# Second attention of a two-layer block: exponentials in a cycle of three tiles, value groups issued several steps later

## The chip, the cores and the metric

The kernel runs on 1 core of one Trainium2 chip. The metric is the device time of the whole program in microseconds (us). Of the core's engines this case concerns PE (TensorE, matrix products), DVE (VectorE), ACT (ScalarE) and SP (SyncE, which only issues DMAs here).

## The reference

The input is 4 batches of 512 tokens with 256 features. Each of two layers normalises the tokens, runs an attention and a mixture of experts on them, and adds both to the tokens. The change concerns the attention of the second layer, a grouped attention with 8 groups of keys and values, 4 query heads per group, and 8 features per head:

```python
q = q.reshape(Bx, Sx, N_GROUPS, R, HEAD_DIM).transpose(0, 2, 3, 1, 4)
k = k.reshape(Bx, Sx, N_GROUPS, HEAD_DIM).transpose(0, 2, 1, 3)
v = v.reshape(Bx, Sx, N_GROUPS, HEAD_DIM).transpose(0, 2, 1, 3)
sim = jnp.einsum('bgrsd,bgtd->bgrst', q, k) / math.sqrt(HEAD_DIM)
attn = jax.nn.softmax(sim, axis=-1)
out = jnp.einsum('bgrst,bgtd->bgrsd', attn, v)
```

With 4 batches and 8 groups there are 32 pairs (b, g). Each needs 4 heads x 512 queries x 512 keys of scores, their maxima over the keys, exponentials, and the product with the values.

## The kernel before

The second attention is one pipeline of stages, written out by hand. Stage (b, s) works on several groups at once: the scores of group s, the exponentials of group s-1, and the outputs of group s-2. Stage (b, 8) and (b, 9) take the scores of groups 0 and 1 of the next batch, so that the program runs through the stages (0,0) to (0,9), (1,2) to (1,9), (2,2) to (2,9), (3,2) to (3,8). A stage has 16 steps. The instructions of each engine run in the order in which they are written; semaphores order the engines against each other.

What PE issues in a stage, by its helper and its line:

- `scores` (L812), one matmul (128 queries x 512 keys) in each of the 16 steps. I call them S0 to S15. DVE takes the maximum of each with one reduction (L1690).
- `maxima_t` (L848), four transposes of the maxima of group s-1 (I call it MX), issued at the step `turn["maxima"]`. DVE adds the result to the stacked queries, `qm` (L1683).
- `scores_t` (L821), items ST0 to ST7 of group s-1: two matmuls each, the scores with the keys on the partitions and the maxima already subtracted. ACT turns each item into exponentials with one ACTIVATE (L1198), E0 to E7. Two items fill one tile `pt[t]`.
- `values` (L833), groups V0 to V3: V_t multiplies tile t of exponentials with the values, 4 matmuls per group (8 records in the trace), and adds up in PSUM bank 7. After V3, ACT copies bank 7 to `ot` (`outputs`, the COPY at L992).
- `outputs_t` (L841), four transposes of `ot` (OUT), issued at the step `turn["outputs"]`. DVE then divides by the sums: a reciprocal and a product (L1660, L1662; I call the pair N).
- In stages 5, 6 and 7 of batches 0 to 2, at step 13, `project` (L539 to L541), six matmuls for the next batch. ACT adds the bias (`compact`, L1171, or L1174 and L1176 for the keys) and DVE makes the low part (L1646, L1649). In stage 9, `values_by_key` (L804) transposes the values of the next batch.

Two tables say at which step the items of a group are issued, counted from the first step of the stage in which its exponentials begin; steps from 16 on fall into the next stage:

```python
            TRANSPOSED = (4, 6, 7, 8, 11, 13, 15, 17)
            VALUED = (10, 15, 19, 19)
```

Three resources couple the engines. PSUM banks 0 to 2 are a ring (`next_bank`) that scores, MX, OUT, projection and `values_by_key` take in PE's order; each use waits until DVE has read the use three places before it. ST items alternate between two pairs of banks, so item i waits for exponential i-2. And the exponentials of tile t may be written only when the value group that read this buffer before is done.

Small steps of the routing of the second layer (masks and slots) are spread over DVE's order in the stages of batch 0, and GpSimd dispatches tokens during the later batches.

Of the kernel before, what the change touches and what calls it, by code (L numbers as in the profile page):

```python
# [7 lines left out]
P = 128  # L8
B, S, H = 4, 512, 256
# [3 lines left out]
QT = S // P  # L13
# [16 lines left out]
NG, R, HD = 8, 4, 8  # L30
# [11 lines left out]
def program(nc, x_in, aw0_in, aw1_in, ws0_in, moe0_in, moe1_in, pad_in, const_in, bias_in, out):  # L42
# [3 lines left out]
    with ctx:  # L46
# [9 lines left out]
        SM, M = 4096, 6688  # L56
# [137 lines left out]
        va = tf(QT, NG, 32)  # L194
        pt = [tf(R, S) for _ in range(2)]
        ot = tf(S)
# [101 lines left out]
        def turns(s, following):  # L298
            never = QT * R
            return {"maxima": 1, "outputs": 6, "values": 4 if s == NG + 1 else never,  # L300
                    "project": 13 if following and NG - 3 <= s < NG else never}
# [235 lines left out]
        def _(pe):  # L537
# [287 lines left out]
            def values(b, g, t):  # L825

                pe.wait_ge(b_ex, b * (2 * NQ) + ((g * QT + t) * 2 + 2))
                if t == 0 and g >= 1:
                    pe.wait_ge(b_ot, b * NG + g)
                if t == 0 and g % NG == 0:  # L830
                    pe.wait_ge(b_va, b + (g // NG + 1))
                for r in range(R):
                    ins = nc.tensor.matmul(psum[32 * r:32 * r + 32, 7, :], va[:, t, g % NG, :], pt[t % 2][:, r, :],  # L833
                                           start=(t == 0), stop=(t == QT - 1), tile_position=(0, 32 * r))
                ins.then_inc(b_pv, 1)
# [16 lines left out]

            TRANSPOSED = (4, 6, 7, 8, 11, 13, 15, 17)
            VALUED = (10, 15, 19, 19)

# [134 lines left out]
        def _(act):  # L990
# [194 lines left out]
            def stage(b, s, last):  # L1185
                back, following = s >= 1, not last and s >= 1
                if s >= 2:
                    outputs(b, s - 2)
                for t in range(QT):
                    if isinstance(b, int) and (b, s, t) == (0, 2, 1):  # L1190
                        gating_exp(E1, 2, TT)
                    if back:
                        g = s - 1
                        for h in range(2):
                            act.wait_ge(b_st, b * (2 * NG * QT) + ((g * QT + t) * 2 + h + 1))
                            if g * QT + t >= 2:
                                act.wait_ge(b_pv, b * (NG * QT) + (g * QT + t - 1))
                            nc.scalar.activation(pt[t % 2][:, 2 * h:2 * h + 2, :], psum[:, 3 + 2 * h:5 + 2 * h, :],  # L1198
                                                 ACT.Exp, scale=float(HD) ** -0.5).then_inc(b_ex, 1)
# [658 lines left out]
```

## Time and profile before

| | |
|---|---|
| median of 3 runs | 1185.54 us |
| lowest, highest | 1183.62, 1187.75 us |
| profiled execution, its own time | 1182.18 us |
| span of the profiled execution | 1180.4 us |
| second attention in it (first MX to last value group) | 501.86 to 963.97 us |
| an ordinary stage (MX to MX) | 13.5 us |
| mean granted TensorE clock | 0.956 of full speed |

The profile lists, for each engine, how long instructions were recorded as busy, and what ended each idle stretch ("idle before <-releaser"). Records of matmuls overlap, since they are pipelined; the time that one really takes from the next is the distance of their starts. In the timelines, equal instructions that follow each other stand in one row with a count, and the row's start is that of the first.

### The profile page before, as it was taken

What the parts mean: (1) busy time and instruction counts of PE and PEld (TensorE: products, weight loads), DVE (VectorE), ACT (ScalarE), POOL (GpSimd) and SP (SyncE); (2) the same over time, 40 slices, a digit from 0 to 9 for tenths busy, and PEclk for the clock granted to TensorE, in tenths of its full rate; (3) what the DMA queues carried; (4) which work ended last, traced back from release to release, by engine and by line L of the source; (5) the groups of instructions that cost most, each with busy time, mean ns of one, the idle gap of its engine ahead of it and who ended that gap; (6) DMA issues with size and microseconds to landing.
All of it is one profiled execution on the core that took longest, in us unless ns stands there. A gap on an engine that the chain in (4) does not pass through costs nothing.

```text
span 1180.4 us, 17538 instructions
## 1 busy us (share of the span) xinstructions
PE 1031.3 (87%) x5780; PEld 744.3 (63%) x5780; DVE 764.5 (65%) x1591; ACT 606.1 (51%) x911; POOL 317.1 (27%) x331
## 2 busy tenths in 40 slices
PE   4979697578999938699998999999999997999996
PEld 3867576467999924455454555555555555888885
DVE  6585254446665525789888878888888837444438
ACT  6325244246555543356665665666656665544431
POOL 2003678125674420000000011221221000455442
PEclk9999899789999969799999999999999998999999
DMA  6862233344444354012111113221222206333243
GB/s 229 311 269 81 94 110 123 104 130 128 154 128 130 117 213 143 7 31 33 17 29 27 27 48 61 54 64 41 59 59 59 65 3 204 100 106 106 86 183 147
DMA packets 49140, 120.49 MB, mean 102 GB/s; under 512 B 7752, under 2 KB 24904, under 8 KB 48520
## 3 DMA queue, kind: packets, MB, share of 16 engines
q1 hardware_dynamic: 36096, 82.80, 24.5%
q0 software_dynamic: 11808, 32.37, 7.2%
q10 hardware_dynamic: 1152, 4.19, 0.9%
q8 instruction: 52, 0.85, 0.3%
q14 instruction: 32, 0.26, 0.1%
HBM read 72.30 MB, written 52.42 MB: 106 GB/s over the span
## 4 chain that ended last, share of the span: by engine, by line
PE 69%; DVE 16%; issue 4%; ACT 4%; DMA 3%; another core or an unknown queue 2%; POOL 1%; SPq 0%; ACTq 0%; DVEq 0%; POOLq 0%
PE psum L812 11%; PE psum L833 9%; PE psum L821 6%; PE psum L539 5%; PE psum L541 5%; PE psum L625 4%; DVE work_f L1690 4%; PE psum L540 4%; PE psum L626 4%; PE psum L627 4%; PE psum L611 2%; PE psum L636 2%; DVE x L1305 1%; PE psum L848 1%
## 5 line engine op out<-in xcount | busy, mean ns | idle before, releaser
L1690 DVE TENSOR_REDUCE work_f<-psum 128x1 f32<-128x512 f32 x512 | 335.5, 685 | 66.8 <-PE psum L812 60.0
L1198 ACT ACTIVATE work_f<-psum 128x1024 f32<-128x1024 f32 x256 | 252.9, 1025 | 122.6 <-PE psum L821 85.5
L812 PE MATMUL psum<-work_r 128*128 128x512 f32 x512 | 201.4, 445 | 24.4 <-DVE work_f L1690 9.5
L476 POOL DMA_INDIRECT yk<-yb,dest x134 | 131.3, 980 | 243.9 <-ACT yb L1052 211.9
L812 PEld LDWEIGHTS psum<-work_r 128*128 128x128 f32 x512 | 92.1, 190 | 148.3 <-DVE work_f L1690 57.6
L821 PE MATMUL psum<-qm,work_r 128*128 128x512 f32 x512 | 163.5, 401 | 1.2 <-ACT work_f L1198 1.2
L469 POOL DMA_INDIRECT xg<-xn,slot x112 | 108.3, 967 | 188.3 <-PE psum L848 150.2
L833 PE MATMUL psum<-work_f 128*32 128x512 f32 x1024 | 131.6, 608 | 0.6 <-ACT work_f L1198 0.5
L625 PE MATMUL psum<-wexp,xbh 128*128 x268 | 102.6, 383 | 7.5 <-issue 7.5
L821 PEld LDWEIGHTS psum<-qm,work_r 128*128 128x128 f32 x512 | 91.6, 189 | 21.5 <-ACT work_f L1198 8.3
L626 PE MATMUL psum<-wexp,xbh 128*128 x268 | 96.4, 360 | 0.0
L627 PE MATMUL psum<-wexp,xbl 128*128 x268 | 95.9, 358 | 0.0
L1474 DVE TENSOR_TENSOR xbl<-psum,xbh 128x512 fp32r<-128x512 f32 x67 | 46.3, 690 | 63.3 <-ACT xbh L992 63.0
L1052 ACT ACTIVATE yb<-psum,share 128x256 f32<-128x256 f32 x134 | 56.3, 472 | 54.3 <-PE psum L653 29.2
L1037 ACT ACTIVATE sgb<-psum 128x352 f32<-128x352 f32 (+1 forms) x67 | 34.8, 519 | 91.1 <-PE psum L627 85.9
L1484 DVE TENSOR_TENSOR hb<-sgb,psum 128x352 f32<-128x352 f32 (+1 forms) x67 | 39.1, 584 | 51.2 <-ACT sgb L1037 45.7
L625 PEld LDWEIGHTS psum<-wexp,xbh 128*128 128x128 f32 x268 | 51.9, 194 | 14.8 <-issue 10.7
L833 PEld LDWEIGHTS psum<-work_f 128*32 128x32 f32 x1024 | 23.4, 109 | 52.7 <-issue 29.0
L611 PE MATMUL psum<-const,xb 128*128 128x128 f32 x268 | 41.8, 280 | 16.9 <-DVE xbl L1474 11.0
L465 POOL TENSOR_TENSOR xn<-const 128x16 f32<-128x16 f32 x7 | 1.5, 220 | 202.2 <-PE psum L848 193.5
L627 PEld LDWEIGHTS psum<-wexp,xbl 128*128 128x128 f32 x268 | 52.0, 194 | 5.1
L626 PEld LDWEIGHTS psum<-wexp,xbh 128*128 128x128 f32 x268 | 52.0, 194 | 3.7
(215 smaller groups left out, 2011.4 us busy)
## 6 DMA issues: line engine op xcount, KB each, us to landing
xb<-xg SPq DMA_DIRECT2D x67, 258.0 KB
xg<-in_pad SPq DMA_DIRECT2D x1, 10320.0 KB
yg<-yk SPq DMA_DIRECT2D x20, 512.0 KB, 9.0
stage<-in_moe SPq DMA_DIRECT2D x16, 608.0 KB
xg<-in_pad SPq DMA_DIRECT2D x1, 7224.0 KB
work_r<-work_r SPq DMA_DIRECT2D x128, 48.0 KB
work_r<-work_r SPq DMA_DIRECT2D x32, 192.0 KB
stage<-in_moe SPq DMA_DIRECT2D x16, 384.0 KB, 4.0
```

The source lines that it names most:

```text
L469: nc.gpsimd.indirect_dma_start(xg[l], bass.IndirectOffsetOnAxis(ap=slot[l][:, at:at + 1], axis=0), xn[l][:, t, :], None).then_inc(m_scat, 16)
L476: nc.gpsimd.indirect_dma_start(yk[l], bass.IndirectOffsetOnAxis(ap=dest[:, j % 8, i:i + 1], axis=0), yb[l][:, j % 2, i, :], None).then_inc ...
L539: nc.tensor.matmul(o, w_hi, x_hi, start=first, stop=False)
L611: ins = nc.tensor.transpose(psum[:, 4, (i * KH + c) * P:(i * KH + c + 1) * P], xb[l][:, j % 2, i, c * P:(c + 1) * P], ident)
L625: nc.tensor.matmul(o, xbh[l][:, j % 2, i * KH + c, :], hi, start=c == 0, stop=False)
L626: nc.tensor.matmul(o, xbh[l][:, j % 2, i * KH + c, :], lo, start=False, stop=False)
L627: ins = nc.tensor.matmul(o, xbl[l][:, j % 2, i * KH + c, :], hi, start=False, stop=c == KH - 1)
L812: nc.tensor.matmul(next_bank(pe, ("scores", n), b_mx, n + 1), qs[g % 2][:, t * P:(t + 1) * P], km[g % 4][:, r, :], start=True, stop=True). ...
L821: ins = nc.tensor.matmul(psum[:, 3 + 2 * h + r % 2, :], km[g % 4][:, r, t * P:(t + 1) * P], qm[g % 2], start=True, stop=True)
L833: ins = nc.tensor.matmul(psum[32 * r:32 * r + 32, 7, :], va[:, t, g % NG, :], pt[t % 2][:, r, :], start=(t == 0), stop=(t == QT - 1), tile ...
L1198: nc.scalar.activation(pt[t % 2][:, 2 * h:2 * h + 2, :], psum[:, 3 + 2 * h:5 + 2 * h, :], ACT.Exp, scale=float(HD) ** -0.5).then_inc(b_ex, 1)
L1690: v.reduce_max(mx[:, s % 2, i:i + 1], ring["scores", n], AX.X).then_inc(b_mx, 1)
```

## The change

Four things change, all in the second attention.

- A third tile of exponentials, `pt2`, is placed in SBUF. Tiles are taken in a cycle of 3 over all groups (tile number modulo 3), and an exponential waits for the value group of the tile three before it instead of two before it.
- The value groups are issued later: V0 at step 15 instead of 10, V1 at 15 as before, V2 at 19 as before, V3 at 25 instead of 19. The ST items get the steps 4, 5, 8, 11, 12, 13, 16, 17.
- MX moves from step 1 to step 2, OUT from step 6 to step 11, `values_by_key` from step 4 to step 12. DVE's counterparts (`qm`, N, the copy of the values) move with them, since they are placed relative to the same numbers.
- On ACT the copy of bank 7 stands between E2 and E3 (t = 1, h = 1) instead of ahead of E0.

```diff
--- before.py
+++ after.py
@@ -192,7 +192,7 @@
         qm = [qm_both[:, n, :] for n in range(2)]
         kv = tf(S)
         va = tf(QT, NG, 32)
-        pt = [tf(R, S) for _ in range(2)]
+        pt = [tf(R, S), tf(R, S), place("pt2", M + 32848, [P, R, S])]
         ot = tf(S)
         mx = tf(2, QT * R)
         rec = tf(QT * R)
@@ -297,7 +297,7 @@
 
         def turns(s, following):
             never = QT * R
-            return {"maxima": 1, "outputs": 6, "values": 4 if s == NG + 1 else never,
+            return {"maxima": 2, "outputs": 11, "values": 12 if s == NG + 1 else never,
                     "project": 13 if following and NG - 3 <= s < NG else never}
 
 
@@ -830,7 +830,7 @@
                 if t == 0 and g % NG == 0:
                     pe.wait_ge(b_va, b + (g // NG + 1))
                 for r in range(R):
-                    ins = nc.tensor.matmul(psum[32 * r:32 * r + 32, 7, :], va[:, t, g % NG, :], pt[t % 2][:, r, :],
+                    ins = nc.tensor.matmul(psum[32 * r:32 * r + 32, 7, :], va[:, t, g % NG, :], pt[((b * NG + g) * QT + t) % 3][:, r, :],
                                            start=(t == 0), stop=(t == QT - 1), tile_position=(0, 32 * r))
                 ins.then_inc(b_pv, 1)
 
@@ -850,8 +850,8 @@
 
 
 
-            TRANSPOSED = (4, 6, 7, 8, 11, 13, 15, 17)
-            VALUED = (10, 15, 19, 19)
+            TRANSPOSED = (4, 5, 8, 11, 12, 13, 16, 17)
+            VALUED = (15, 15, 19, 25)
 
             def follow(b, g, step):
                 for n in range(2 * QT):
@@ -1184,18 +1184,18 @@
 
             def stage(b, s, last):
                 back, following = s >= 1, not last and s >= 1
-                if s >= 2:
-                    outputs(b, s - 2)
                 for t in range(QT):
                     if isinstance(b, int) and (b, s, t) == (0, 2, 1):
                         gating_exp(E1, 2, TT)
                     if back:
                         g = s - 1
                         for h in range(2):
+                            if s >= 2 and (t, h) == (1, 1):
+                                outputs(b, s - 2)
                             act.wait_ge(b_st, b * (2 * NG * QT) + ((g * QT + t) * 2 + h + 1))
-                            if g * QT + t >= 2:
-                                act.wait_ge(b_pv, b * (NG * QT) + (g * QT + t - 1))
-                            nc.scalar.activation(pt[t % 2][:, 2 * h:2 * h + 2, :], psum[:, 3 + 2 * h:5 + 2 * h, :],
+                            if b * (NG * QT) + g * QT + t >= 3:
+                                act.wait_ge(b_pv, b * (NG * QT) + (g * QT + t - 2))
+                            nc.scalar.activation(pt[((b * NG + g) * QT + t) % 3][:, 2 * h:2 * h + 2, :], psum[:, 3 + 2 * h:5 + 2 * h, :],
                                                  ACT.Exp, scale=float(HD) ** -0.5).then_inc(b_ex, 1)
                     if t == 2 and following and NG - 3 <= s < NG:
                         compact((0, 2, 1)[s - (NG - 3)], b + 1, ring["projection", b * 3 + s - (NG - 3) + 4], s - (NG - 3))
```

PE at the border of stages (1,4) and (1,5), before. L833 is a value group of 4 matmuls (`work_f_147` holds the tiles `pt[0]` and `pt[1]` and the values), L812 the scores, L821 the ST items, L848 is MX:

```order
L812 MATMUL psum<-work_r_146 128x512 x2
L821 MATMUL psum<-qm,work_r_146 128x512 x2
L833 MATMUL psum<-work_f_147 32x512 x4
L812 MATMUL psum<-work_r_146 128x512 x2
L848 MATMUL psum<-const,work_r_146 128x128 x4
L821 MATMUL psum<-qm,work_r_146 128x512 x2
L812 MATMUL psum<-work_r_146 128x512 x2
L833 MATMUL psum<-work_f_147 32x512 x8
```

And now:

```order
L812 MATMUL psum<-work_r_146 128x512 x2
L833 MATMUL psum<-pt_149,work_f_147 32x512 x4
L833 MATMUL psum<-work_f_147 32x512 x4
L812 MATMUL psum<-work_r_146 128x512
L821 MATMUL psum<-qm,work_r_146 128x512 x2
L812 MATMUL psum<-work_r_146 128x512
L821 MATMUL psum<-qm,work_r_146 128x512 x2
L812 MATMUL psum<-work_r_146 128x512
L848 MATMUL psum<-const,work_r_146 128x128 x4
L812 MATMUL psum<-work_r_146 128x512
L833 MATMUL psum<-work_f_147 32x512 x4
```

V0 has moved down to stand directly ahead of V1, ST6 and ST7 stand in the first two steps of the next stage, MX comes after S2, and only V2 follows it where V2 and V3 stood together. `pt_149` is the new tile.

PE in the middle of stage (1,4), steps 4 to 11, before. L841 is OUT:

```order
L812 MATMUL psum<-work_r_146 128x512
L821 MATMUL psum<-qm,work_r_146 128x512 x2
L812 MATMUL psum<-work_r_146 128x512 x2
L821 MATMUL psum<-qm,work_r_146 128x512 x2
L841 MATMUL psum<-const,work_f_147 128x128 x4
L812 MATMUL psum<-work_r_146 128x512
L821 MATMUL psum<-qm,work_r_146 128x512 x2
L812 MATMUL psum<-work_r_146 128x512
L821 MATMUL psum<-qm,work_r_146 128x512 x2
L812 MATMUL psum<-work_r_146 128x512 x2
L833 MATMUL psum<-work_f_147 32x512 x4
L812 MATMUL psum<-work_r_146 128x512
```

And now:

```order
L812 MATMUL psum<-work_r_146 128x512
L821 MATMUL psum<-qm,work_r_146 128x512 x2
L812 MATMUL psum<-work_r_146 128x512
L821 MATMUL psum<-qm,work_r_146 128x512 x2
L812 MATMUL psum<-work_r_146 128x512 x3
L821 MATMUL psum<-qm,work_r_146 128x512 x2
L812 MATMUL psum<-work_r_146 128x512
L833 MATMUL psum<-work_f_147 32x512 x4
L812 MATMUL psum<-work_r_146 128x512 x2
L821 MATMUL psum<-qm,work_r_146 128x512 x2
L841 MATMUL psum<-const,work_f_147 128x128 x4
L812 MATMUL psum<-work_r_146 128x512
```

V3 of the group before stands in the middle of the stage, after S9, where before V0 stood after S10; OUT has moved from behind ST1 to behind ST3.

ACT from the copy of stage (1,4) to the projection in stage (1,5), before. L992 is the copy, L1198 the exponentials, L1171 the bias of the projection:

```order
L992 COPY work_f_147<-psum 128x512
L1198 ACTIVATE work_f_147<-psum 128x1024 x8
L992 COPY work_f_147<-psum 128x512
L1198 ACTIVATE work_f_147<-psum 128x1024 x6
L1171 ACTIVATE work_r_146<-psum,bias 128x512 x2
L1198 ACTIVATE work_f_147<-psum 128x1024 x2
```

And now, from the exponential E2 of stage (1,4) on:

```order
L1198 ACTIVATE work_f_147<-psum 128x1024
L992 COPY work_f_147<-psum 128x512
L1198 ACTIVATE work_f_147<-psum 128x1024 x3
L1198 ACTIVATE pt_149<-psum 128x1024 x2
L1198 ACTIVATE work_f_147<-psum 128x1024 x3
L992 COPY work_f_147<-psum 128x512
L1198 ACTIVATE work_f_147<-psum 128x1024
L1198 ACTIVATE pt_149<-psum 128x1024 x2
L1171 ACTIVATE work_r_146<-psum,bias 128x512 x2
L1198 ACTIVATE work_f_147<-psum 128x1024 x4
```

The copy stands after the third exponential of a stage, and the tiles alternate with `pt_149` every third time. SP's and GpSimd's instructions stand as before.

## Rows read from the trace of the kernel before

**Rows 1.** the page: shares by engine of the chain that ended last
```profile
PE 69%; DVE 16%; issue 4%; ACT 4%; DMA 3%; another core or an unknown queue 2%; POOL 1%; SPq 0%; ACTq 0%; DVEq 0%; POOLq 0%
```

**Rows 2.** windows, a stage each: us, then PE, PEld, DVE, ACT, POOL busy, clock, DMA
```profile
540.88:554.63 13.75, 13.58 (x73) 6.97 (x72) 12.83 (x46) 8.49 (x10) 0.00 (x0) 1.00 0.19 29
...
616.64:632.84 16.20, 14.35 (x78) 7.35 (x77) 15.17 (x38) 9.24 (x10) 0.00 (x0) 1.00 0.15 24
632.84:649.97 17.13, 15.33 (x72) 7.29 (x73) 13.41 (x28) 7.82 (x9) 0.00 (x0) 0.90 0.15 24
...
663.49:677.00 13.51, 13.41 (x73) 7.05 (x72) 11.61 (x22) 8.47 (x10) 0.00 (x0) 1.00 0.19 29
...
808.40:824.34 15.94, 14.78 (x78) 8.17 (x78) 12.31 (x23) 10.33 (x12) 2.89 (x3) 1.00 0.13 37
824.34:839.76 15.42, 14.78 (x79) 8.18 (x79) 12.38 (x23) 9.76 (x11) 3.31 (x5) 1.00 0.36 66
...
sum 447.77, PE 430.87 PEld 228.99 DVE 376.97 ACT 274.21 POOL 47.50; mean PE 13.90 PEld 7.39 DVE 12.16 ACT 8.85 POOL 1.53
```

**Rows 3.** timeline of PE in stages (1,4) and (1,5): start us, us, instruction, count
```profile
678.75 1.92 PE L833 MATMUL psum<-work_f 128*32 128x512 f32 x16
680.61 0.50 PE L812 MATMUL psum<-work_r 128*128 128x512 f32 x1
680.95 0.63 PE L821 MATMUL psum<-qm,work_r 128*128 128x512 f32 x2
681.41 0.63 PE L812 MATMUL psum<-work_r 128*128 128x512 f32 x2
681.87 0.63 PE L821 MATMUL psum<-qm,work_r 128*128 128x512 f32 x2
682.34 0.60 PE L841 MATMUL psum<-const,work_f 128*128 128x128 f32 x4
682.70 0.48 PE L812 MATMUL psum<-work_r 128*128 128x512 f32 x1
...
683.71 0.64 PE L821 MATMUL psum<-qm,work_r 128*128 128x512 f32 x2
684.44 0.74 PE L812 MATMUL psum<-work_r 128*128 128x512 f32 x2
685.11 1.07 PE L833 MATMUL psum<-work_f 128*32 128x512 f32 x8
686.10 0.50 PE L812 MATMUL psum<-work_r 128*128 128x512 f32 x1
```

**Rows 4.** timeline of DVE, same stretch
```profile
676.97 1.29 DVE L1690 TENSOR_REDUCE work_f<-psum 128x1 f32<-128x512 f32 x2 [0.26 <-PE psum L812]
678.18 0.68 DVE L1683 TENSOR_TENSOR qm<-psum,work_r 128x512 fp32r<-128x512 f32 x1
...
681.15 2.75 DVE L1690 TENSOR_REDUCE work_f<-psum 128x1 f32<-128x512 f32 x4 [1.09 <-PE psum L812]
683.82 0.25 DVE L1660 RECIPROCAL work_f<-psum 128x16 f32<-128x16 f32 x1
684.10 0.29 DVE L1662 TENSOR_TENSOR on<-psum,work_f 128x128 f32<-128x128 f32 x1
```

**Rows 5.** timeline of ACT, same stretch
```profile
680.74 0.59 ACT L992 COPY work_f<-psum 128x512 f32<-128x512 f32 x1 [1.61 <-PE psum L833]
681.61 4.00 ACT L1198 ACTIVATE work_f<-psum 128x1024 f32<-128x1024 f32 x4 [0.28 <-PE psum L821]
...
689.42 1.27 ACT L1171 ACTIVATE work_r<-psum,bias 128x512 fp32r<-128x512 f32 x2 [0.37 <-PE psum L541]
```

**Rows 6.** timeline of PE behind the projection of stage (1,5)
```profile
691.62 0.70 PE L812 MATMUL psum<-work_r 128*128 128x512 f32 x2 [0.31 <-DVE work_r L1646]
```

**Rows 7.** timeline at the end of the attention
```profile
947.16 0.76 PE L812 MATMUL psum<-work_r 128*128 128x512 f32 x2
...
962.97 1.06 PE L833 MATMUL psum<-work_f 128*32 128x512 f32 x8 [0.46 <-ACT work_f L1198]
```

## The prediction

> **What bounds the kernel now.** I read the page's chain first: 69% of it lies on PE and 16% on DVE [rows 1]. Then the windows, cut from one MX to the next, so that each is a stage: 31 of them take 447.8 us of the span [rows 2]. An ordinary stage takes 13.51 us, and in it ACT is busy for 8.5 and DVE for 11.6 [rows 2]. A stage with a projection takes 15.4 to 15.9 [rows 2]; there are 9 of these. PE is recorded as busy for 13.41 of 13.51 [rows 2], which looks full. The Trainium skill warns of this reading (Perfetto Trace Analysis, Identifying the Most-Contended Engine): matmul busy time is no measure of headroom, since pipelined matmuls overlap in the record. By the busy row the change could win 0.1 us a stage, 3 us in all; by the distances of starts it can win more, and the starts decide.
>
> The starts give what each item takes from the next [rows 3]: a score 0.23 us in a dense run (two in 0.46 between 681.41 and 681.87), but 0.34 when it follows a value group or a wait (680.61 to 680.95); an ST item 0.46; OUT or MX 0.36; two value groups together 1.86, one alone 0.99 with the change of mode around it. A stage has 16 scores, 8 ST items, 4 value groups, MX and OUT. Added up with these prices it is about 12.6 us. So PE stands still for 0.9 us of an ordinary stage, in pieces: 0.27 behind ST3 (683.71 plus 0.46 is 684.17, the next score starts at 684.44), and the rest at S2, S3, S10 and S15.
>
> On DVE two reductions run in 1.21 us (676.97 to 678.18), so one costs 0.60 although it is recorded as 0.69 [rows 4]. `qm` costs about the same, N 0.57 up to its end at 684.39; the score that waits for it starts 0.05 later [rows 3, 4]. DVE needs some 11.0 us of 13.5. It loses 1.09 us at 681.15 [rows 4]: it has eaten its three banks while PE was in the block V2, V3. That starvation makes the ring late for the rest of the stage, and PE then waits for DVE at S9. So the two engines wait for each other in turn; neither is full.
>
> **The change, step by step.** It adds no instruction and removes none. I lay an ordinary stage out, with the prices above, time 0 at S0. A score may start 0.74 us after the start of the reduction that frees its bank (record 0.69, plus 0.05); a reduction starts 0.44 us after its score, 0.54 after a score that follows a value group (680.61 to 681.15) [rows 3, 4]; an exponential starts 0.66 after its ST item (680.95 to 681.61), and four of them take 4.00 [rows 3, 5].
>
> PE: S0 0, ST6 0.34, S1 0.80, ST7 1.03, S2 1.50, MX 1.73 (it now needs the bank of S0; that reduction runs from 0.54, so the bank is free at 1.28), S3 2.09, V2 2.42, S4 3.42, ST0 3.76 (needs `qm`, which ends at 3.2), S5 4.22, ST1 4.45, S6 and S7 from 4.92, S8 5.40, ST2 5.63, S9 6.10, V3 6.43, S10 7.43, S11 7.77, ST3 8.00, OUT 8.47, S12 8.83, ST4 9.14, S13 9.60, ST5 9.83. S14 needs N. DVE reaches N at 9.95 (reduction 12 starts at 9.34), and N is over at 10.52, so S14 starts at 10.57 where it could have at 10.29. S15 10.91, V0 and V1 from 11.24, and the next S0 at 13.10. The stage is 13.10 against 13.51: 0.41 less.
>
> Why the pieces hold. The block of two value groups is not gone, it has moved behind S15. There three reductions and the two small negations (about 2.1 us of work from the end of N on) lie beside it; the first result of the next stage comes 3.1 us behind the end of N, so DVE starves for about 1.0 us there. But it is the only place: behind V2 and V3, each alone now, DVE has results in hand, and of the 1.09 ahead of S4's reduction and the 0.26 at the start of a stage [rows 4] only the second is left, grown to 1.0. ACT's copy starts 0.13 behind V3 (at 680.74 behind the block that ends at 680.61 [rows 3, 5]), here at 7.56, and ends at 8.15, ahead of OUT at 8.47; behind it in ACT's queue stands E3, which cannot start before 8.66 (ST3 plus 0.66), so the copy costs nothing there. E3 ends at 9.7 and ST5 needs it at 9.83: the cover is 0.1 us, and 0.3 more before S14 would move. The third tile is what lets E4 and E5 run without V0: they wait for V3 of the group before, which ended at 7.43. Without it V0 could not stand at step 15. SP's keys and queries are loaded when ST7 and `qm` of an earlier group are over; those come about 1 us later in a stage and are needed a stage later, so the queue has the slack.
>
> A projection stage. Before, the projection's bank is read by ACT (0.37 behind its last matmul, 1.27 us for two) [rows 5] and then DVE, and the next S0 needs that bank: it starts only at 691.62, and the row names DVE's L1646 as what it waited for [rows 6]. Before, only S14, S15, ST6 and V1 lay beside that chain. Now: the projection must wait for N and starts at 10.57, S14 11.98, S15 12.21, V0 and V1 12.54 to 14.40. ACT's two copies run from 12.16 to 13.43, DVE's part from 13.46 to 14.2. The bank is free before S0 wants it at 14.40. Stage: 14.40, against 15.42 [rows 2], 1.0 less. The three uses of the ring are the same. For the keys ACT needs one copy more, 0.6 us, so DVE is over at 14.8: stage 14.79 against 15.94 [rows 2], 1.15 less. Over the 9 stages, 1.1 each, 9.9 us.
>
> Stage 9 of batches 1 and 2, with `values_by_key`: S13 waits for N, S15 for DVE's copy; laid out in the same way, it wins 0.35: 0.7 for the two. Batch 0: in stages 3 and 4 the routing steps fill DVE (12.83 of 13.75 [rows 2]); only its starvation shrinks (there the routing steps lie beside the double block too), 0.2 each. In stage 9 DVE is busy for 15.17 of 16.20 and in (1,2) PE waits for a run of routing steps and drops to a granted clock of 0.90 in the mean [rows 2]; the run itself stays. I take 1.2 us off for both together, 0 to 3 as bounds. The end: after the last scores at 947.16 the last value group starts at 962.97 [rows 7]. There the exponentials set the pace; the copy now stands in their row (0.59 more), but ST0 comes after one value group instead of two (0.9 less), and ST6 waits behind V0, V1. Laid out, 0.6 less in sum; I bound it by 1 either way.
>
> The sum: 16 ordinary stages x 0.41 = 6.6; projections 9.9; stage 9 twice 0.7; batch 0 0.4 + 1.2; end 0.6. That is 19.4 us. The profiled execution took 1182.2 us, its span 1180.4; it lies 3.4 under the median of the three runs, 1185.5. Nothing behind the attention changes, so it moves as a whole: 1162.8 against the profiled execution, 1166.1 against the median. I predict 1166. The prices are good to about 0.15 us a stage (the 0.1 that a wait adds, the start of N), 31 stages, 5 us; with the bounds of batch 0 and of the end the forecast's own range is 1160 to 1173.
>
> **The rivals.** (a) The projection stages gain little. ACT comes to the bias late, since E5 stands ahead of it and now ends near 11.7, just under the 12.16 at which the projection can be read. If it ended 1 us later, S0 would wait again and the 9 stages would keep 0.8 us each: 1173. Against it: the 0.5 us to spare; for it: that ACT's queue is dense there. 0.12.
>
> (b) Nothing changes. If DVE's reduction really costs what is recorded (0.69) when it isn't starved, a stage needs 17 x 0.69 + N + the negations = 12.6, and with 0.7 of starvation it is 13.3: 0.2 x 16, or some 3 us; the same number as by PE's busy row. The time would be 1182, which isn't to be told from no change. Against it stand the 1.21 us for two [rows 4]. 0.11.
>
> (c) Slower. The exponentials come late: E3 now stands behind E2 and the copy, and ST5, S14 and the double block hang on E3. If E2 were not begun when V3 ends, E2, copy and E3 would run in a row and E3 would end at 10.2, 0.4 late for ST5. It decides from 0.7 us of delay on (0.3 of cover and the 0.41 gained). At 1.2 us late, 0.5 us would be lost in 22 stages, 11 us: 1197. E2 starts 0.66 behind ST2, at 6.3, so V3 would have to be early or ST2 late by over 1 us. 0.05.
>
> **Chances.** The forecast 0.72, (a) 0.12, (b) 0.11, (c) 0.05. The forecast and (a) are faster; a measurement tells this kernel's change from none at about 0.3%, 3.6 us, so (b) is the same. Faster 0.84, same 0.11, slower 0.05. The range holds the forecast and (a) with the error of the prices: 1159 to 1178.
>
> **What would show it.** In the new profile an ordinary stage should be 13.1 from MX to MX, a projection stage 14.4 (keys 14.8). DVE's idle of 1.09 behind S4 should be gone and one of about 1 us stand ahead of the first reduction of a stage. PE's wait for L1646 should be gone or short, and its waits for N (L1662) should stand at S14. ACT's copy should start 0.13 behind a single value group. I am wrong if PE waits for L1198 at ST5 in every stage, if reductions run at 0.69 from start to start with results at hand, or if the clock falls in more stages than (1,2).

## The result and the profile after

The changed kernel takes 1167.65 us (median of 4 runs, 1164.3 to 1169.57), the kernel before 1184.81 (4 runs beside it, 1183.62 to 1187.75). The ratio is 0.985, 95% interval [0.982, 0.988]. The profiled execution took 1164.3 us, 17.9 less than that of before, its span 1162.5 at the same mean clock (0.955). On the page the chain has 70% on PE and 16% on DVE, as in [rows 1].

Windows from MX to MX, as in [rows 2]. The stages are (0,9), (1,2), (1,3), (2,7) with a projection, and the sum of 31:

```profile
612.97:630.22 17.25, 14.69 (x78) 7.60 (x76) 16.44 (x43) 9.78 (x11) 0.00 (x0) 1.00 0.14 23
630.22:643.62 13.40, 13.30 (x72) 7.18 (x73) 11.95 (x22) 7.25 (x8) 0.00 (x0) 1.00 0.20 31
643.62:656.85 13.23, 13.13 (x73) 7.13 (x72) 11.79 (x22) 8.46 (x10) 0.00 (x0) 1.00 0.20 32
...
812.04:826.74 14.70, 14.61 (x79) 8.29 (x79) 12.30 (x23) 9.72 (x12) 3.30 (x5) 1.00 0.35 67
...
sum 431.81, PE 422.63 PEld 232.76 DVE 377.67 ACT 273.48 POOL 47.41; mean PE 13.63 PEld 7.51 DVE 12.18 ACT 8.82 POOL 1.53
```

The sum fell from 447.77 us to 431.81, by 16.0. An ordinary stage went from 13.49–13.54 to 13.23–13.27, one with the keys from 15.94 to 15.16, the projection of (2,7) from 15.42 to 14.70. (0,9) became longer, 16.20 to 17.25, and (1,2) went from 17.13 to 13.40 with the clock now at 1.00 throughout. From the last MX to the transposes that follow the attention it was 14.34 us, now it is 13.15.

PE at the border of batch 0 (first row), in an ordinary stage from S0 of (1,4) to S0 of (1,5), and from the projection of (1,5) on, as [rows 3, 6] (the stretch in [rows 3] lies in (1,5), ahead of its projection, where the stage is still like an ordinary one):

```profile
630.22 0.63 PE L848 MATMUL psum<-const,work_r 128*128 128x128 f32 x4 [1.06 <-DVE work_f L1690]
...
655.13 0.50 PE L812 MATMUL psum<-work_r 128*128 128x512 f32 x1
...
657.21 0.48 PE L812 MATMUL psum<-work_r 128*128 128x512 f32 x1
657.62 1.06 PE L833 MATMUL psum<-work_f 128*32 128x512 f32 x8
...
660.12 0.98 PE L812 MATMUL psum<-work_r 128*128 128x512 f32 x3
660.60 0.19 PEld L812 LDWEIGHTS psum<-work_r 128*128 128x128 f32 x1 [0.29 <-DVE work_f L1690]
660.94 0.63 PE L821 MATMUL psum<-qm,work_r 128*128 128x512 f32 x2
...
661.73 1.07 PE L833 MATMUL psum<-work_f 128*32 128x512 f32 x8
...
665.13 0.65 PE L821 MATMUL psum<-qm,work_r 128*128 128x512 f32 x2
665.87 0.74 PE L812 MATMUL psum<-work_r 128*128 128x512 f32 x2
666.53 1.06 PE L833 MATMUL psum<-pt,work_f 128*32 128x512 f32 x8
...
668.38 0.50 PE L812 MATMUL psum<-work_r 128*128 128x512 f32 x1
...
679.13 0.50 PE L539 MATMUL psum<-xt_hi,aw 128*128 128x512 f32 x1
...
680.64 0.63 PE L812 MATMUL psum<-work_r 128*128 128x512 f32 x2
...
683.05 0.50 PE L812 MATMUL psum<-work_r 128*128 128x512 f32 x1
```

V2 (657.62) and V3 (661.73) stand alone, V0 (666.53) and V1 together, and the next S0 (668.38) behind them. The row of PEld is the weight load of S8, the third of the three scores at 660.12. ST5 starts at 665.13 and takes 0.46, so PE would be free for S14 at 665.59; S14 starts at 665.87. That is the wait of 0.28 for N. Behind the projection, S0 (683.05) follows V0 and V1 with no wait in its row, where [rows 6] had 0.31 for L1646.

DVE in the same two places, as [rows 4]:

```profile
655.66 2.08 DVE L1690 TENSOR_REDUCE work_f<-psum 128x1 f32<-128x512 f32 x3 [0.81 <-PE psum L812]
...
659.15 3.88 DVE L1690 TENSOR_REDUCE work_f<-psum 128x1 f32<-128x512 f32 x6 [0.22 <-PE psum L812]
663.26 2.06 DVE L1690 TENSOR_REDUCE work_f<-psum 128x1 f32<-128x512 f32 x3 [0.22 <-PE psum L812]
...
665.52 0.29 DVE L1662 TENSOR_TENSOR on<-psum,work_f 128x128 f32<-128x128 f32 x1
...
682.14 0.75 DVE L1646 SCALAR_TENSOR_TENSOR work_r<-psum,bias,work_r 128x512 fp32r<-128x512 f32 x1 [0.38 <-ACT work_r L1171]
```

The idle time of 1.09 behind S4 is now 0.22 (659.15), and 0.81 stands ahead of the first reduction of a stage (655.66). N (L1662) ends at 665.81, S14 starts 0.06 later. In the projection stage DVE's L1646 ends at 682.89, 0.16 ahead of S0.

ACT, as [rows 5]:

```profile
662.86 0.59 ACT L992 COPY work_f<-psum 128x512 f32<-128x512 f32 x1 [0.23 <-PE psum L833]
663.96 3.07 ACT L1198 ACTIVATE work_f<-psum 128x1024 f32<-128x1024 f32 x3 [0.52 <-PE psum L821]
```

The copy starts 1.13 behind the start of V3, 0.14 behind its end (a value group alone takes 0.99), and E3 (663.96) waits for ST3, not for the copy.

DVE's idle time ahead of all the reductions of the program, on the page of the kernel before and then on that of the kernel after (busy, mean ns of one | idle before):

```profile
L1690 DVE TENSOR_REDUCE work_f<-psum 128x1 f32<-128x512 f32 x512 | 335.5, 685 | 66.8 <-PE psum L812 60.0
```

```profile
L1690 DVE TENSOR_REDUCE work_f<-psum 128x1 f32<-128x512 f32 x512 | 337.0, 685 | 48.9 <-PE psum L812 46.4
```

66.8 us became 48.9. DVE does the same work, and its idle time ahead of it is 17.9 us shorter; 13.6 of these were waits put down to PE's scores (60.0, now 46.4). That the span fell by 17.9 as well proves nothing by itself: idle time of DVE counts only where PE then waits for DVE.

### The profile page after: what moved, and what is told of

It is laid out like the page before. It is cut to its first block, busy times and chain, and to the rows that moved or that the text cites. A ratio compares the mean times of both kernels' runs of the same rounds, so it can differ in the third digit from the quotient of the medians.

```text
span 1162.5 us, 17536 instructions
## 1 busy us (share of the span) xinstructions
PE 1023.0 (88%) x5780; PEld 748.4 (64%) x5780; DVE 764.7 (66%) x1591; ACT 605.1 (52%) x911; POOL 317.6 (27%) x331
## 4 chain that ended last, share of the span: by engine, by line
PE 70%; DVE 16%; issue 4%; ACT 3%; DMA 3%; another core or an unknown queue 2%; POOL 1%; SPq 0%; ACTq 0%; DVEq 0%; POOLq 0%
PE psum L812 10%; PE psum L833 9%; PE psum L821 7%; DVE work_f L1690 6%; PE psum L539 5%; PE psum L541 5%; PE psum L540 5%; PE psum L625 5%; PE psum L626 4%; PE psum L627 4%; PE psum L611 2%; PE psum L636 2%; PE psum L657 1%; DVE x L1305 1%
## 5 line engine op out<-in xcount | busy, mean ns | idle before, releaser
L1690 DVE TENSOR_REDUCE work_f<-psum 128x1 f32<-128x512 f32 x512 | 337.0, 685 | 48.9 <-PE psum L812 46.4
L1198 ACT ACTIVATE work_f<-psum 128x1024 f32<-128x1024 f32 x172 | 169.5, 1024 | 104.9 <-PE psum L821 100.6
L812 PE MATMUL psum<-work_r 128*128 128x512 f32 x512 | 207.6, 444 | 18.7 <-DVE work_f L1690 6.8
L812 PEld LDWEIGHTS psum<-work_r 128*128 128x128 f32 x512 | 93.4, 190 | 133.5 <-DVE work_f L1690 70.7
L821 PE MATMUL psum<-qm,work_r 128*128 128x512 f32 x512 | 160.8, 396 | 0.9 <-ACT work_f L1198 0.8
L821 PEld LDWEIGHTS psum<-qm,work_r 128*128 128x128 f32 x512 | 93.8, 188 | 24.0 <-ACT work_f L1198 6.2
L1198 ACT ACTIVATE pt<-psum 128x1024 f32<-128x1024 f32 x84 | 82.8, 1023 | 45.8 <-PE psum L821 42.7
L833 PE MATMUL psum<-work_f 128*32 128x512 f32 x688 | 89.1, 602 | 0.6 <-ACT work_f L1198 0.6
L625 PEld LDWEIGHTS psum<-wexp,xbh 128*128 128x128 f32 x268 | 51.8, 193 | 14.6 <-issue 10.3
```

The lines of the kernel that those rows point to most:

```text
L625: nc.tensor.matmul(o, xbh[l][:, j % 2, i * KH + c, :], hi, start=c == 0, stop=False)
L812: nc.tensor.matmul(next_bank(pe, ("scores", n), b_mx, n + 1), qs[g % 2][:, t * P:(t + 1) * P], km[g % 4][:, r, :], start=True, stop=True). ...
L821: ins = nc.tensor.matmul(psum[:, 3 + 2 * h + r % 2, :], km[g % 4][:, r, t * P:(t + 1) * P], qm[g % 2], start=True, stop=True)
L1198: nc.scalar.activation(pt[((b * NG + g) * QT + t) % 3][:, 2 * h:2 * h + 2, :], psum[:, 3 + 2 * h:5 + 2 * h, :], ACT.Exp, scale=float(HD) * ...
L1690: v.reduce_max(mx[:, s % 2, i:i + 1], ring["scores", n], AX.X).then_inc(b_mx, 1)
```

## The experiments

Each experiment is the changed kernel with the edit shown. They ran in three groups, each on another chip: on one of them the kernel before takes 1157.3 us, on the other two 1180.5 and 1180.8, so times are compared as ratios to the kernel before on the same chip. Stages of the attention can be compared directly: the changed kernel was profiled on two chips, and its 31 stages agree to 0.05 us, but for (2,8) (13.56 and 13.28).

### The third tile alone

```diff
-            return {"maxima": 2, "outputs": 11, "values": 12 if s == NG + 1 else never,
+            return {"maxima": 1, "outputs": 6, "values": 4 if s == NG + 1 else never,
...
-            TRANSPOSED = (4, 5, 8, 11, 12, 13, 16, 17)
-            VALUED = (15, 15, 19, 25)
+            TRANSPOSED = (4, 6, 7, 8, 11, 13, 15, 17)
+            VALUED = (10, 15, 19, 19)
...
+                if s >= 2:
+                    outputs(b, s - 2)
...
-                            if s >= 2 and (t, h) == (1, 1):
-                                outputs(b, s - 2)
```

> The kernel before with the third tile of exponentials and the wait on the tile three before, all steps as before. My theory (the gain comes from where PE's value groups stand against DVE's reductions): in the kernel before PE never waits for E6 or E7, which are the exponentials that the third tile frees, so the time stays at that of before, 1181 to 1188. Rival (the exponentials were held up by their two tiles, and the third tile is the gain): 1168 to 1178.

Measured: 1182.67 us (9 runs) beside 1180.53 (21 runs), ratio 1.002 [1.000, 1.003]. Ordinary stages take 13.49 to 13.54, as before. The tile by itself gives nothing; the gain is in the order.

### The new order with two tiles

```diff
-        pt = [tf(R, S), tf(R, S), place("pt2", M + 32848, [P, R, S])]
+        pt = [tf(R, S), tf(R, S)]
...
-                            if b * (NG * QT) + g * QT + t >= 3:
-                                act.wait_ge(b_pv, b * (NG * QT) + (g * QT + t - 2))
+                            if b * (NG * QT) + g * QT + t >= 2:
+                                act.wait_ge(b_pv, b * (NG * QT) + (g * QT + t - 1))
```

(and `pt[t % 2]` in `values` and in the exponential.)

> The changed kernel with two tiles and the wait on the tile two before. By the layout of a stage: E4 now waits for V0, which ends near 12.4 of the stage, so E5 ends at 14.5, ST7 waits 0.3 us in every stage, and in the 9 projection stages the bias copies stand behind E5 on ACT, so that the bank is free only at 16.6 and S0 waits some 2 us: 9 plus 19 us on the changed kernel, 1188 to 1198, slower than before. Rival (the third tile is idle comfort): 1164 to 1170.

Measured: 1241.27 us (5 runs), ratio 1.052 [1.050, 1.054]. It is slower, as expected, but by 61 us where I had some 10. ACT in an ordinary stage:

```profile
672.83 1.03 ACT L1198 ACTIVATE work_f<-psum 128x1024 f32<-128x1024 f32 x1 [1.35 <-PE psum L833]
...
678.41 3.79 ACT L1198 ACTIVATE work_f<-psum 128x1024 f32<-128x1024 f32 x4 [3.15 <-PE psum L833]
```

I had counted only E4's wait for V0 (here 3.15 us of idle time at 678.41). E2 waits too: it writes tile 1, which V3 of the group before reads, and V3 now stands at step 9. E2 starts at 672.83, when that group is over, with an idle of 1.35; the copy (673.75) and E3 follow in a row, and OUT waits 0.54 us for the copy:

```profile
674.38 0.66 PE L841 MATMUL psum<-const,work_f 128*128 128x128 f32 x4 [0.54 <-ACT work_f L992]
```

An ordinary stage takes 14.4, a projection stage 19.4 to 21.1. The nine projection stages hold the larger part, 50 of the 77 us that the 31 stages take more than in the changed kernel. E4 and E5 stand behind V0, the bias behind E5, and S0 behind both; I had laid its wait out as 2 us, and it is 3.29 (3.81 with the keys):

```profile
712.66 0.47 PE L812 MATMUL psum<-work_r 128*128 128x512 f32 x1 [3.29 <-DVE work_r L1646]
```

So the third tile frees E2 and E3 from V3 of the group before, as well as E4 and E5 from V0. The order costs 61 us without it and gains 17 with it.

### V3 back beside V2

```diff
-            VALUED = (15, 15, 19, 25)
+            VALUED = (15, 15, 19, 19)
```

> The changed kernel with V3 back at step 19, directly behind V2; V0, V1, tiles, ST items, MX, OUT and ACT's order stay as changed. My theory (the block V2, V3 starves DVE by 1.1 us and makes the ring late for the rest of the stage): DVE's idle of 1.1 us ahead of the reduction of S4 comes back and an ordinary stage goes from 13.25 to 13.4 to 13.5: 1171 to 1176. Rival (the gain comes from the other moves: ST items, OUT, or the double block beside the projection): 1165 to 1169 with stages of 13.25.

Measured: 1180.91 us (12 runs), ratio 1.001 [1.000, 1.003]. Ordinary stages take 13.70, 0.45 more than in the changed kernel and 0.2 more than before. I had expected some of the gain to stay, and in the sum none did. It did in the nine projection stages, which take 15.1 to 15.9: they keep 3.3 of their 8.1 us, and the ordinary ones lose 6.7, more than they had gained. DVE:

```profile
658.18 2.09 DVE L1690 TENSOR_REDUCE work_f<-psum 128x1 f32<-128x512 f32 x3 [0.80 <-PE psum L812]
...
662.53 5.75 DVE L1690 TENSOR_REDUCE work_f<-psum 128x1 f32<-128x512 f32 x9 [1.06 <-PE psum L812]
```

The starvation behind V2 and V3 is back (1.06), and the one at the start of a stage has not gone (0.80). The order with V0 behind S15 has one block of two already; with V3 at step 3 it has two of them.

### V0 at step 13

```diff
-            VALUED = (15, 15, 19, 25)
+            VALUED = (13, 15, 19, 25)
```

> The changed kernel with V0 at step 13 instead of 15, so that no two value groups are neighbours and V0 fills PE's wait for N. By the layout: an ordinary stage gains 0.05 us (13.2; the wait of 0.28 is filled, one more change between scores and values costs 0.17), and a projection stage loses 0.5 to 0.9, since the projection comes 0.7 later and one value group less stands beside ACT's and DVE's work on it: 1169 to 1175. Rival (DVE's starvation behind the double block, 0.81 us a stage, is what bounds the stage now): 1150 to 1162.

Measured: 1173.84 us (5 runs), ratio 0.995 [0.993, 0.996]. The time lies in the range that I gave, but only because the kernel before is faster on this chip: against the 1184.8 for which the range was meant, it is a ratio of 0.987 to 0.992, and the measured one is above it. The 31 stages take 11 us more than in the changed kernel, where I expected 1 to 7. Ordinary stages came as expected (13.20). What is lost lies in the projection stages, 15.4 to 16.0 instead of 14.6 to 15.2 since V0 no longer covers the bias (PE waits 0.8 us for L1646 where it waited for nothing, and 1.3 for L1649 where it waited 0.44), in stage 9 of the later batches (15.07 instead of 14.62), and at the border of batch 0: (0,9) takes 18.61 and (1,2) 14.96. The last two, 3.8 us together, I had not counted. So V0's place behind S15 is worth about 0.8 us in each of 9 projection stages and nothing in the 16 ordinary ones.

### ST items at their old steps

```diff
-            TRANSPOSED = (4, 5, 8, 11, 12, 13, 16, 17)
+            TRANSPOSED = (4, 6, 7, 8, 11, 13, 15, 17)
```

> The changed kernel with the ST items back at steps 4, 6, 7, 8, 11, 13, 15, 17. Theory (the ST items are cover, not work that was saved): ST3 at step 8 has to wait for E1, about 0.2, and the double block comes after ST6, so one item less stands behind it ahead of MX; ordinary stages 13.3 to 13.5, 2 to 8 us slower than the changed kernel: 0.985 to 0.992 of the kernel before. Rival (the new places of the ST items carry a large part of the gain): 0.995 or more.

Measured: 1171.78 us (4 runs) beside 1157.33 (9 runs), ratio 1.013 [1.011, 1.014]. My theory fell: the ST steps aren't a detail. Undoing them alone costs 30 us, twice what the whole change gains on this chip, and undoing V3's move alone also took the whole gain; the parts work together and can't be added up. An ordinary stage takes 14.29, 1.05 more than in the changed kernel and 0.8 more than before. DVE:

```profile
640.41 1.89 DVE L1690 TENSOR_REDUCE work_f<-psum 128x1 f32<-128x512 f32 x3 [1.25 <-PE psum L812]
...
648.61 2.06 DVE L1690 TENSOR_REDUCE work_f<-psum 128x1 f32<-128x512 f32 x3 [0.73 <-PE psum L812]
```

DVE starves 1.25 at the start of a stage, since ST6 now stands between S15 and V0 and makes the next S0 come 0.46 later, and again 0.73 at 648.61, behind V3: in steps 6 to 8 each score stands beside an ST item, and DVE has nothing in hand when V3 starts. ACT shows a third place:

```profile
648.21 0.59 ACT L992 COPY work_f<-psum 128x512 f32<-128x512 f32 x1 [1.16 <-PE psum L833]
648.70 1.95 ACT L1198 ACTIVATE work_f<-psum 128x1024 f32<-128x1024 f32 x2
```

ST3 is now issued ahead of V3, at 646.18, and could be read at 646.84. But the copy stands ahead of E3 in ACT's queue and waits for V3, so E3 starts only at 648.70. How the 1.05 divides among the three was not measured apart.

### MX back at step 1

```diff
-            return {"maxima": 2, "outputs": 11, "values": 12 if s == NG + 1 else never,
+            return {"maxima": 1, "outputs": 11, "values": 12 if s == NG + 1 else never,
```

> The changed kernel with MX back at step 1 instead of step 2. Theory: MX needs only bank space and the two small negations, which end 0.3 us ahead of S0, so it can start 0.7 earlier; S2 would then take the bank of S0, free 1.3 behind S0 and wanted at 1.9, so nothing waits, and DVE has the same number of results to eat. The starvation of 0.81 at the start of a stage stays. Ordinary stage 13.2 to 13.3, as in the changed kernel, and the ratio to the kernel before 0.984 to 0.988. Rival: step 2 is part of the gain, since two scores ahead of MX give DVE results for longer while the value group V2 follows; then a stage with MX at step 1 is 0.1 to 0.3 longer, and the ratio 0.989 to 0.993.

Measured: 1165.49 us (6 runs) beside 1180.79 (11 runs), ratio 0.987 [0.984, 0.990]. Ordinary stages take 13.23 to 13.26. The step of MX makes no difference there. OUT at step 11 was not tried apart; it can't stand ahead of V3 and the copy.

### ACT's copy ahead of E2

```diff
-                            if s >= 2 and (t, h) == (1, 1):
+                            if s >= 2 and (t, h) == (1, 0):
```

> The changed kernel with ACT's copy of bank 7 one exponential earlier, ahead of E2 instead of behind it. The copy waits for V3, which ends 7.6 behind the S0 of an ordinary stage, so E2, that ran from 6.5 to 7.5 beside V3, must now follow the copy: copy, E2, E3 in a row, the chain of rival (c). In the trace of the changed kernel the copy runs from 662.86 to 663.45 and E3 from 663.96; now E2 would run from 663.5 to 664.5 and E3 to 665.5, 0.55 later than before. ST5 starts at 665.13 and needs E3, so it would start near 665.6, and S14 near 666.05 instead of 665.87. Theory (the cover at ST5 is 0.1 us, and S14's wait for N takes up 0.3 more): an ordinary stage becomes 0.15 to 0.3 longer, 13.4 to 13.5, a projection stage by about as much, and the time 5 to 9 us above the changed kernel, ratio to the kernel before 0.990 to 0.994. Rival (the exponentials have slack, since they are busy for 8.5 of 13.2): no stage moves by more than 0.05, ratio 0.985 to 0.987. Against both: more than 0.5 a stage, if E2's delay holds back ST4 and what is behind it in PE's order as well.

Measured: 1162.84 us (5 runs), ratio 0.985 [0.983, 0.987], and ordinary stages of 13.22 to 13.27: the chain of rival (c) is there, and costs nothing. ACT and then PE:

```profile
666.39 3.79 ACT L1198 ACTIVATE work_f<-psum 128x1024 f32<-128x1024 f32 x4
```

```profile
658.17 0.50 PE L812 MATMUL psum<-work_r 128*128 128x512 f32 x1
...
668.39 0.73 PE L821 MATMUL psum<-qm,work_r 128*128 128x512 f32 x2
668.96 0.67 PE L812 MATMUL psum<-work_r 128*128 128x512 f32 x2
```

The copy (0.59, from 665.91) and the exponentials from E2 on stand in a row. ST5 starts 10.22 behind S0 (658.17), in the changed kernel 10.00, so it is 0.22 late. But S14 starts at 10.79, there at 10.74: the delay goes into the wait for N, which is there anyway. I had put E3 0.55 late, taking the recorded 1.02 for each exponential; the four here start 0.92 apart (3.79 in all), so E3 starts 9.14 behind S0, in the changed kernel 8.83: it is late by 0.3.

### N one reduction earlier

OUT's result is there when DVE has reduced S11, but N was written behind the reduction of S12. S14 takes OUT's bank, so PE waits for N there.

```diff
-                    if i == turn["outputs"] + 1 and s >= 2:
+                    if i == turn["outputs"] and s >= 2:
```

> The changed kernel with DVE's N (reciprocal and product) after the reduction of S11 instead of S12. By the layout S14 no longer waits 0.28 for N, but S15 then waits for the reduction of S12, which is one N later, so ordinary stages stay at 13.2 to 13.3; in the 9 projection stages the projection starts 0.28 earlier and the stage is 0.2 to 0.3 shorter: 2 to 3 us faster than the changed kernel, 0.981 to 0.984 of the kernel before. Rival (OUT isn't ready when DVE gets to N, and DVE waits): same as changed or slower.

The changed kernel itself was run again beside it:

> The changed kernel as it is, beside the variants. 0.982 to 0.987 of the kernel before. If the clock at the border of stages (0,9) and (1,2) follows from PE's idle there (1.06 us) and not from chance, the clock stays at full speed there in this profile too, and stage (1,2) takes 13.4; if chance decides, it may show the 17 us of the kernel before.

Measured, with N earlier: 1131.74 us (5 runs) beside 1157.33, ratio 0.978 [0.977, 0.979]. The changed kernel: 1141.94 us (5 runs), 0.987 [0.985, 0.989]; at the border of (0,9) and (1,2) its granted clock is again 1.00, behind an idle of 1.09, and (1,2) takes 13.42. So the full clock there was no accident of one profile.

So this one line takes 10 us more off, and it beats both kernels. It beats what I expected of it too: an ordinary stage takes 12.88, 0.35 less, where my layout had S15 wait for the reduction of S12 in its turn. Windows, PE and DVE:

```profile
616.13:629.01 12.88, 12.88 (x74) 7.21 (x73) 11.62 (x22) 8.47 (x10) 0.00 (x0) 1.00 0.21 32
```

```profile
624.38 0.64 PE L821 MATMUL psum<-qm,work_r 128*128 128x512 f32 x2
624.86 0.62 PE L812 MATMUL psum<-work_r 128*128 128x512 f32 x2
625.41 1.06 PE L833 MATMUL psum<-work_f 128*32 128x512 f32 x8
...
627.27 0.50 PE L812 MATMUL psum<-work_r 128*128 128x512 f32 x1
```

```profile
624.22 2.47 DVE L1690 TENSOR_REDUCE work_f<-psum 128x1 f32<-128x512 f32 x4
```

S14 starts at 624.86, 0.48 behind ST5, with no wait, and V0 0.55 later, where it was 0.66 behind a score that had waited. The reduction of S12 runs from 624.22, right behind N, so its bank is free at about 624.96, before S15 wants it. PE is recorded as busy for the whole of an ordinary stage, and no matmul row in it names a wait. A small one is left all the same: the weight load of S8 starts only at 619.86, when its bank is free, and S6, S7 and S8 take 0.83 (619.37 to 620.20).

### N earlier, and V0 at step 14 where there is no projection

```diff
-                    if VALUED[t] == step:
+                    if (VALUED[t] if t or (b < B - 1 and 4 <= g < 7) else 14) == step:
...
-                    if i == turn["outputs"] + 1 and s >= 2:
+                    if i == turn["outputs"] and s >= 2:
```

> As the one before, and V0 at step 14 in all stages without a projection, 15 in those with one. V0 then fills PE's wait for the reduction of S12, and DVE is starved less behind V1: ordinary stages 13.1 to 13.2 instead of 13.25, 1 to 2 us faster than the one before, 0.979 to 0.983 of the kernel before. Rival (as in the kernel with V0 at 13, PE's idle at the border of (0,9) and (1,2) grows and the clock falls there): 0 to 1 us slower.

Measured: 1136.25 us (5 runs), ratio 0.982 [0.980, 0.984]: 4.5 us slower than with V0 behind S15, not faster. Ordinary stages take 13.20. PE:

```profile
628.55 0.39 PE L812 MATMUL psum<-work_r 128*128 128x512 f32 x1
628.87 1.07 PE L833 MATMUL psum<-work_f 128*32 128x512 f32 x8
629.86 0.51 PE L812 MATMUL psum<-work_r 128*128 128x512 f32 x1
630.30 1.07 PE L833 MATMUL psum<-pt,work_f 128*32 128x512 f32 x8
631.29 0.50 PE L812 MATMUL psum<-work_r 128*128 128x512 f32 x1
```

From S14 to the next S0 it is 2.74 (628.55 to 631.29), with both groups behind S15 2.41 (624.86 to 627.27). No matmul row in either stretch names a wait. The difference is the price of the change between scores and value groups: S14 to V0 0.32, V0 to S15 0.99, S15 to V1 0.44, V1 to S0 0.99, against 0.55 for two scores and 1.86 for two groups. Once PE has hardly a wait left, what counts is how often it changes between scores and value groups.

### Stage length against starvation

One ordinary stage of each kernel, with the idle time that DVE's timeline lists ahead of its reductions:

| kernel | stage us | DVE idle us | difference |
|---|---|---|---|
| before | 13.51 | 0.26 + 1.08 + 0.37 = 1.71 | 11.80 |
| after | 13.23 | 0.81 + 0.22 + 0.22 = 1.25 | 11.98 |
| V3 beside V2 | 13.70 | 0.80 + 1.06 = 1.86 | 11.84 |
| V0 at 13 | 13.20 | 0.21 + 0.23 + 0.82 = 1.26 | 11.94 |
| old ST steps | 14.29 | 1.25 + 0.22 + 0.24 + 0.73 = 2.44 | 11.85 |
| N earlier | 12.88 | 0.70 + 0.20 + 0.23 = 1.13 | 11.75 |
| N earlier, V0 at 14 | 13.20 | 0.21 + 0.23 + 0.62 + 0.31 = 1.37 | 11.83 |

The last column stays within 0.23 while the stage moves by 1.4. The idle time is a good index of what an order is worth here. In part that is arithmetic: DVE has the same work in each of these stages, so the difference is that work and the gaps too small to be listed. Nor is the idle time the cause by itself: DVE starves because PE's scores come in the wrong places, and in the last two kernels PE sets the pace with hardly a wait.

## Why the prediction was right

It said 1166.0; the median is 1167.65. By its own steps:

| term | forecast us | measured us |
|---|---|---|
| 16 ordinary stages | 6.6 | 4.5 |
| 9 projection stages | 9.9 | 8.1 |
| stage 9 of batches 1 and 2 | 0.7 | 0.1 |
| stages (0,3), (0,4) | 0.4 | 0.7 |
| (0,9) and (1,2) | 1.2 | 2.7 |
| the end | 0.6 | 1.2 |
| sum | 19.4 | 17.2 |

The profiled execution gained 17.9; the remaining 0.7 lies behind the attention (from the transposes to the end of the span 216.4 us before, 215.7 after).

The mechanism was right, and the sum came so close partly by luck: the first three terms were 4.5 us too high, and the border and the end gave back 2.1, most of it through a clock that I had not looked at.

**Ordinary stages.** The mechanism held: the waits stand where the layout put them. The wait for N is 0.28 (forecast 0.28), and behind V0 and V1 DVE starves for 0.8 (forecast 1.0). The stage is 13.25 from S0 to S0 and not 13.10, and all of that is there before V3 (6.60 against 6.43). Two prices were too low. (In all that follows S0 is at 655.13.) From S3, behind MX, to V2 it takes 0.41 (657.21 to 657.62), where I had 0.33. And S6, S7 and S8 take 0.82 to ST2 instead of 0.71. DVE had starved 0.22 at S4's result, where I had said it had results in hand, and takes S5 only when it comes (659.86, 0.44 behind S5 at 659.42); S8 takes the bank of S5, and its weight load starts at 660.60, 0.74 behind that reduction. My layout had the bank free just when S8 wanted it (5.40). So it was wrong that the start of the stage is "the only place" of starvation; there are two small ones of 0.22 as well. The sixteen are also less alike than "16 x" says: eleven gained 0.24 to 0.31 each, (3,7) 0.76, (2,8) 0.68, (0,8) 0.26, (1,8) 0.09, and (0,1) lost 0.38.

**Projection stages.** 14.62 to 14.71 (the first, in batch 0, 15.03) against the forecast of 14.40, and 15.16 with the keys against 14.79. They carry the same 0.17, and the six matmuls take 1.51 (679.13 to 680.64), not 1.41. The term looks better than it was: the nine took 141.9 us before, more than 15.42 and 15.94 each, so my own lengths of 14.40 and 14.79 would have given 11.2, not 9.9; measured are 8.1. I also misread a row: the 0.37 at the bias in [rows 5] is ACT's idle time, not its distance from the last matmul, which is 0.43 from start to start; the layout's 12.16 doesn't rest on it. The margin of rival (a) was as thin as I said: DVE's part ends 0.16 ahead of S0 (forecast 0.2). With the keys, PE still waits for DVE's L1649, 1.3 us in three stages (before 2.5 in three); for L1646 it waits no more. The experiment with V0 at 13 shows this cover at work.

**Stage 9 of batches 1 and 2.** The term that failed outright, if small: 14.65 and 14.67 became 14.61 and 14.62. I had laid the wait for DVE's copy of the values (L1653) out as short; PE waits 0.4 us for it once in each batch, where before it waited 0.51 for the same copy at OUT. And S13 waits 0.38 for N. So one wait replaced another. PE's idle time ahead of scores in the attention of the kernel after, by releaser (us in all, times):

```profile
L812 PE MATMUL psum<-work_r x495: 387/397/505, 500.8 to 930.4; 128*128 128x512 f32 x165
...
  DVE work_f L1653: 1.2, 3
```

**The border of batch 0.** I said that "the run itself stays" and gave 1.2. The run of routing steps did stay, and (0,9) grew by 1.05. But (1,2) fell by 3.7, since PE's clock didn't fall. Before, PE idles 0.52 and 1.61 us ahead of the score at 635.56, and then the granted clock is 0.58 and V2 and V3 take 3.37 us instead of 1.92 [rows 3]; the two scores ahead of them take 1.21 up to V2, where two take 0.67 up to V0 at the full clock [rows 3]. That is some 2.0 us for the lower clock, and without it the border would have gained about 0.7. PE and then a window of the kernel before:

```profile
632.84 0.66 PE L848 MATMUL psum<-const,work_r 128*128 128x128 f32 x4 [0.52 <-DVE work_r L1704]
...
635.56 1.28 PE L812 MATMUL psum<-work_r 128*128 128x512 f32 x2 [1.61 <-DVE work_f L1690]
636.77 3.37 PE L833 MATMUL psum<-work_f 128*32 128x512 f32 x16
```

```profile
636.00:638.00 2.00, 1.90 (x10) 0.58 (x13) 1.90 (x4) 0.00 (x0) 0.00 (x0) 0.58 0.00 0
```

Now PE idles once, for 1.06 at MX (630.22), and the granted clock stays at 1.00. I had seen the 0.90 and not asked what would become of it.

**The end** gained 1.2 instead of 0.6, inside its bound.

**The rivals.** (b), that nothing changes because a reduction costs what is recorded, is out: the stages fell, and with results at hand four reductions take 2.47 us (at 624.22 with N earlier), 0.60 from start to start. (a) did not come, by 0.16 us. (c) was weaker than I had it: the copy ahead of E2 makes ST5 0.2 late and costs nothing. Its danger lies elsewhere. With two tiles, and with ST3 ahead of V3, E3 does come late, and those kernels are 5% and 1.3% slower than the one before; how much of that is E3's was not measured apart.

## What to carry to other kernels

Where two engines hand each other a short ring of banks, lay the order out by distances of starts and look at both engines' waits; PE was recorded as busy for 13.41 of 13.51 us here, in a stage that could be had in 12.88. Don't put two long items of the producer side by side unless the consumer has work of its own beside them, and move such a block to where the consumer has it, or where a slow hand-over (here the bias) needs cover. Parting two such items has a price too, 0.33 us here (2.74 against 2.41), so it pays only where it removes a wait. When a reordering leaves a wait of known size (here 0.28 for N), ask at once what is queued ahead of its releaser: one line moved up by one reduction was worth 10 us more, over half as much as the whole change.

## What was not expected of the hardware

- A wait, or a change between kinds of matmuls, cost more than the idle time listed for it. The score behind MX takes 0.41 up to the value group, S14 behind an ST item 0.32 (V0 at 14). The pair of scores that waited for N takes 0.66 to V0, without a wait 0.55. So removing a wait of 0.28 shortened a stage by 0.35.
- The granted clock fell to the lower of its two levels after some idle times of PE and not after others, at the same place of the program. It fell with 0.52 and 1.61 us close to each other (before, and the third tile alone) and with 1.98 (V0 at 13), and it stayed with 0.68 to 1.20 in the other nine profiles, among them 1.06 (after), 1.07 (V3 beside V2) and 0.80 (MX at step 1). With V0 at 13 the clock granted in the 2 us from 636 on was 0.50. What decides between the two was not tried.
- One chip runs the kernel before in 1157.3 us, two others in 1180.5 and 1180.8. The stages of the attention are alike in the two profiles of the changed kernel; the first MX starts 477 to 481 us into the span on the one and 498 to 505 on the others, so most of the difference lies ahead of the attention. What sets it was not looked into.
